# Output projection of the last two pairs of heads taken one head later, in a two-layer transformer kernel

## What is computed

```python
# layer 1 attention: x seen as B = 4 sequences of S tokens, H = 32 heads of 128
q = jnp.einsum('bsd,de->bse', hidden_states, wq).reshape(B, S, H, DQ)
scores = jnp.einsum('bqhd,bkhd->bhqk', q[..., :DN], k) * scale     # causal mask
probs = jax.nn.softmax(scores, axis=-1)
attn = jnp.einsum('bhqk,bkhd->bqhd', probs, v).reshape(B, S, H * DV)
return jnp.einsum('bse,ed->bsd', attn, wo)
# after it
x = _layernorm(x + attention(x))
x = _layernorm(x + L1_ffn(x))      # dense matrix plus gated low-rank experts
```

## Time and profile before

| | |
|---|---|
| time, median of 3 runs | 1513.86 us (1513.7 to 1514.61) |
| time of the profiled execution | 1514.25 us |
| its span | 1512.4 us |
| TensorE busy in the span | 1447.8 us, 96% |
| VectorE, ScalarE, GpSimd busy | 1021.7, 899.0, 797.5 us |
| mean granted TensorE clock | 0.985 of full |
| heads 30 and 31 with the epilogue | about 1382 to 1438 us of the span |
| last stage | from 1438.28 us to the end |

### The profile page before, as it was taken

One profiled execution on the slowest core, in us unless ns is written; L12 is line 12 of the kernel. 1 busy time (PEld: TensorE's weight loads), 2 busy tenths in 40 slices (PEclk: granted clock), 3 DMA queues, 4 the chain that ended last, 5 costly groups with the idle time before them and its releaser, 6 DMA issues. The chain is left out here.

```text
span 1512.4 us, 30701 instructions
## 1 busy us (share of the span) xinstructions
PE 1447.8 (96%) x8801; PEld 1267.2 (84%) x8801; DVE 1021.7 (68%) x2484; ACT 899.0 (59%) x2445; POOL 797.5 (53%) x891
## 2 busy tenths in 40 slices
PE   6999999999599988999999999999999999999797
PEld 5898898988377767988898898899889889889686
DVE  3788888888496866566656656656665566566665
ACT  3787878888355536555655655655566555556521
POOL 3455555555241226775756657566565665654421
PEclk9999999999899999999999999999999999999999
DMA  4223232322245410101010010100101011010201
GB/s 166 66 70 88 67 86 72 82 77 65 69 133 161 129 44 28 57 29 56 28 55 28 28 55 28 55 28 30 54 28 55 28 38 45 28 42 14 77 15 42
DMA packets 56196, 88.62 MB, mean 59 GB/s; under 512 B 6112, under 2 KB 31200, under 8 KB 56160
## 3 DMA queue, kind: packets, MB, share of 16 engines
q1 hardware_dynamic: 56160, 88.16, 19.4%
HBM read 77.66 MB, written 2.10 MB: 53 GB/s over the span
## 5 line engine op out<-in xcount | busy, mean ns | idle before, releaser
L1292 POOL TENSOR_TENSOR c_qk<-g_y,c_qk 128x512 fp32r<-128x512 f32 x96 | 124.1, 1293 | 149.5 <-ACT c_qk L1386 149.5
L466 POOL TENSOR_TENSOR h_pr<-h_pr,h_rinv 128x512 f32<-128x512 f32 x128 | 133.3, 1041 | 132.0 <-DVE h_rinv L557 129.6
L1170 POOL TENSOR_TENSOR b_sw_lo<-b_slots,b_sw_hi 128x512 fp32r<-128x512 f32 (+1 forms) x128 | 148.7, 1162 | 10.2
L1168 POOL CAST b_sw_hi<-b_slots 128x512 fp32r<-128x512 f32 (+1 forms) x128 | 73.0, 570 | 134.9 <-DMA b_slots<-in_w_qk 124.0
L98 PE MATMUL c_bv<-b_wv_hi,g_xT_hi 128*128 128x256 f32 x504 | 141.0, 280 | 0.0
L99 PE MATMUL c_bv<-b_wv_lo,g_xT_hi 128*128 128x256 f32 x504 | 140.8, 279 | 0.0
L100 PE MATMUL c_bv<-b_wv_hi,g_xT_lo 128*128 128x256 f32 x504 | 140.7, 279 | 0.0
L1386 ACT ACTIVATE c_qk<-g_y 128x512 fp32r<-128x512 f32 x96 | 61.0, 636 | 106.1 <-DVE g_y L1512 75.2
L496 ACT ACTIVATE h_pr<-h_bs,h_nmax 128x256 f32<-128x256 f32 x256 | 119.0, 474 | 6.4 <-DVE h_nmax L552 3.0
L1486 DVE TENSOR_TENSOR c_bo<-c_bo,g_wo 128x128 f32<-128x128 f32 x128 | 38.4, 300 | 119.0 <-ACT g_wo L1363 119.0
L1353 ACT ACTIVATE c_pr<-c_pr,c_rinv 128x128 f32<-128x128 f32 (+1 forms) x256 | 102.4, 450 | 8.2 <-DVE c_rinv L1476 8.2
(11 more groups left out here) (303 smaller groups left out, 5237.0 us busy)
## 6 DMA issues: line engine op xcount, KB each, us to landing
f_wi<-in_w_ffn SPq DMA_DIRECT2D x66, 256.0 KB, 2.6
b_slots<-in_w_qk SPq DMA_DIRECT2D x64, 256.0 KB, 2.8
h_part<-in_w_ffn SPq DMA_DIRECT2D x32, 264.0 KB, 2.7
h_o_mix<-h_o_hi SPq DMA_DIRECT2D x64, 128.0 KB, 2.2
b_raw_v<-in_w_v SPq DMA_DIRECT2D x16, 512.0 KB, 4.5
b_raw_o<-in_w_o SPq DMA_DIRECT2D x16, 512.0 KB, 4.4
a_w<-in_w_head SPq DMA_DIRECT2D x32, 225.0 KB, 2.6
b_ffn_w<-in_w_ffn SPq DMA_DIRECT2D x4, 576.0 KB, 6.8
```

Source lines behind the costliest of these rows:

```text
L466: pool.tensor_tensor(pr[b][:, :, :], pr[b][:, :, :], rinv[b][:, :][:, :, None].to_broadcast([P, 2, S]), ALU.mult)\
L1168: pool.tensor_copy(self.sw[0][:, a:b], self.slots[:, a:b]).then_inc(self.s_whi, 1)
L1170: pool.tensor_tensor(self.sw[1][:, a:b], self.slots[:, a:b], f32(self.sw[0][:, a:b]), ALU.subtract)\
L1292: pool.tensor_tensor(lo, src, f32(hi), ALU.subtract).then_inc(s_sumlo, 1)
```

## The change

All 16 output tiles of the last two pairs are taken later, in one sequence numbered `n` = 0 to 15 (`late_out`, `late_add`, `late_tile`). Tiles 0 and 1 (of pair 14) come in step 3 of head 30, two in each step of head 31 (2 to 7 of pair 14, 8 and 9 of pair 15), and the six others of pair 15 in the epilogue. Steps 0 to 2 of head 30 have no output tile. The banks rotate over three (`bv`, `by`, `bx`), and a tile waits for the addition of the tile three before it.

As pair 14's result is still needed while pair 15's is written, head 30 writes its result to a new place, `o_last`, which lies under the former `slots`; its first write waits until GpSimd has split the last projection weights. The last pair's output weights go to the buffers of the value weights (`split_last_o`), once all values are made, no longer behind the tiles of pair 14.

ScalarE's `ffn1_hi` pieces move: one after step 1, two after step 2, two after step 3 of head 31, none in the epilogue. VectorE's epilogue puts the statistics of token tiles 0 to 3 between the additions.

```diff
+        last = k.under("o_last", [P, 2, T], F32R)
+        self.o_last = (last[:, 0, :], last[:, 1, :])
...
+    def split_last_o(self, pool, used):
+        pool.wait_ge(self.s_in["o"], 16 * NG)
+        pool.wait_ge(*used)
+        plain(pool, self.g["tick"])
+        hi, lo = self.ws["v"]
+        pool.tensor_copy(hi[:, :], self.raw["o"][:, :]).then_inc(self.s_vohi["v"], 1)
+        pool.wait_ge(self.s_vohi["v"], NG + 1)
+        pool.tensor_tensor(lo[:, :], self.raw["o"][:, :], f32(hi[:, :]), ALU.subtract).then_inc(self.s_volo["v"], 1)
...
+        def home(gr, hd):
+            return self.o_last if is_last_pair(gr) and hd == 0 else tuple(x[:, hd, :] for x in oT)
+        def late_tile(n):
+            return NG - 2 + n // NT, n % NT, (bv, by, bx)[n % 3]
...
-                    if hd == 1 and has(gr, NG):
+                    if hd == 1 and is_last_pair(gr):
+                        self.split_last_o(pool, (s_vmm, 4 * NG))
+                    elif hd == 1 and has(gr, NG):
                         self.split(pool, "o", gr, [(s_omm, 8 * gr)])
...
+                    if to is self.o_last and b == 0:
+                        act.wait_ge(s_wlo, 4 * NH)
...
                         if is_last(gr, hd) and t:
-                            ffn1_hi(act, self.ffn_raw, t - 1)
+                            for c in ((0,), (1, 2), (3, KC))[t - 1]:
+                                ffn1_hi(act, self.ffn_raw, c)
                 def epilogue():
                     out_rest(NSTEP - 1, 3)
-                    outs(NSTEP - 1, 1, 3)
-                    for c in (KC - 1, KC):
-                        ffn1_hi(act, self.ffn_raw, c)
+                    outs(NSTEP - 1, home(NG - 1, 1), 3)
...
-                        if is_last(gr, hd) and t:
+                        if is_last_pair(gr) and (hd == 1 or t == 3):
                             for i in range(2):
-                                j = 2 * t - 2 + i
-                                add_out(8 * gr + j, j, (bx, by)[i])
+                                late_add((2 + 2 * t if hd else 0) + i)
...
                     out_sum(NSTEP - 1, 3)
-                    outs(NSTEP - 1, 1, 3)
-                    for j in range(4):
-                        after.stats(dve, j, (s_oadd, 8 * (NG - 1) + j + 1))
+                    stats(0)
+                    outs(NSTEP - 1, home(NG - 1, 1), 3)
+                    stats(1)
+                    for j in (2, 3):
+                        late_add(NT + j)
+                        stats(j)
                     after.spread(dve, 0)
-                    for i in range(2):
-                        add_out(NT * NG - 2 + i, NT - 2 + i, (bx, by)[i])
+                    for j in late:
+                        late_add(NT + j)
...
                         def tile(i):
+                            if is_last_pair(gr):
+                                if hd == 1 or t == 3:
+                                    late_out((2 + 2 * t if hd else 0) + i)
+                                return
...
-                            if is_last(gr, hd) and t:
-                                n = 8 * gr + 2 * t - 2 + i
-                                pe.wait_ge(s_oadd, n - 1)
-                                pe.wait_ge(s_olo, s)
-                                out(gr, 2 * t - 2 + i, (bx, by)[i])
...
+                def late_out(n):
+                    gr, j, bank = late_tile(n)
+                    if n == 0:
+                        pe.wait_ge(s_vlo, 4 * NG)
+                    elif n == 1:
+                        pe.wait_ge(s_sum, 3 * NH)
+                    elif n == 2:
+                        pe.wait_ge(s_klo, NH)
+                    else:
+                        pe.wait_ge(s_oadd, NT * (NG - 2) + n - 2)
+                    if is_last_pair(gr):
+                        pe.wait_ge(s_olo, NSTEP - 3 + j // 2)
+                    out(gr, j, bank)
+
                 def epilogue():
-                    pe.wait_ge(s_olo, NSTEP)
-                    for i in range(2):
-                        pe.wait_ge(s_oadd, NT * NG - 3 + i)
-                        out(NG - 1, NT - 2 + i, (bx, by)[i])
+                    for j in range(2, NT):
+                        late_out(NT + j)
```

More of the change, by code:

```diff
@@ L1256, in is_last, with is_last_pair @@
             return isinstance(gr, int) and (gr, hd) == (NG - 1, 1)
+        def is_last_pair(gr):
+            return isinstance(gr, int) and gr == NG - 1
+        def home(gr, hd):
+            return self.o_last if is_last_pair(gr) and hd == 0 else tuple(x[:, hd, :] for x in oT)
+        def late_tile(n):
+            return NG - 2 + n // NT, n % NT, (bv, by, bx)[n % 3]
         turned = [bo[0], bo[1], bt, bs[1]]
@@ L1363, in out_rest, with outs @@
                     act.activation(o1, bo[t % 2][:, 2 * P:3 * P], ACT.Identity).then_inc(s_orest, 1)
-                def outs(s, hd, b):
+                def outs(s, to, b):
                     act.wait_ge(s_osum, s + 1)
-                    act.activation(oT[0][:, hd, b * S:(b + 1) * S], bo[b % 2][:, 0:S], ACT.Identity)\
+                    if to is self.o_last and b == 0:
+                        act.wait_ge(s_wlo, 4 * NH)
+                    act.activation(to[0][:, b * S:(b + 1) * S], bo[b % 2][:, 0:S], ACT.Identity)\
                        .then_inc(s_ohi, 1)
@@ L1432, in unit @@
                         if has(s - 1, NSTEP):
-                            outs(s - 1, hd if t else 1 - hd, (t - 1) % 4)
+                            outs(s - 1, home(gr, hd if t else 1 - hd), (t - 1) % 4)
                         if has(s + 1, NSTEP):
@@ L1486, in out_sum, with outs @@
                     dve.tensor_tensor(out, out, o1, ALU.add).then_inc(s_osum, 1)
-                def outs(s, hd, b):
+                def outs(s, to, b):
                     dve.wait_ge(s_ohi, s + 1)
                     tok = slice(b * S, (b + 1) * S)
-                    dve.tensor_tensor(oT[1][:, hd, tok], bo[b % 2][:, 0:S], f32(oT[0][:, hd, tok]), ALU.subtract)\
+                    dve.tensor_tensor(to[1][:, tok], bo[b % 2][:, 0:S], f32(to[0][:, tok]), ALU.subtract)\
                        .then_inc(s_olo, 1)
@@ L1585, in unit @@
                             inverse(s + 1, (t + 1) % 4)
-                        if hd == 0 and has(gr - 1, NG):
+                        regular = hd == 0 and has(gr - 1, NG) and not is_last_pair(gr)
+                        if regular:
                             add_out(8 * (gr - 1) + 2 * t, 2 * t, bv)
@@ L1591, in unit, with late_add, stats @@
                             total(h + 1, t)
-                        if hd == 0 and has(gr - 1, NG):
+                        if regular:
                             add_out(8 * (gr - 1) + 2 * t + 1, 2 * t + 1, bv if t < 3 else by)
-                        if is_last(gr, hd) and t:
+                        if is_last_pair(gr) and (hd == 1 or t == 3):
                             for i in range(2):
-                                j = 2 * t - 2 + i
-                                add_out(8 * gr + j, j, (bx, by)[i])
+                                late_add((2 + 2 * t if hd else 0) + i)
+                def late_add(n):
+                    _, j, bank = late_tile(n)
+                    add_out(NT * (NG - 2) + n, j, bank)
                 def epilogue():
+                    def stats(j):
+                        after.stats(dve, j, (s_oadd, NT * (NG - 1) + j + 1))
                     out_sum(NSTEP - 1, 3)
-                    outs(NSTEP - 1, 1, 3)
-                    for j in range(4):
-                        after.stats(dve, j, (s_oadd, 8 * (NG - 1) + j + 1))
+                    stats(0)
[4 more added lines that the diff above has]
+                        stats(j)
                     after.spread(dve, 0)
-                    for i in range(2):
-                        add_out(NT * NG - 2 + i, NT - 2 + i, (bx, by)[i])
+                    for j in late:
+                        late_add(NT + j)
                 sweep(dve, prologue, unit, epilogue)
@@ L1664, in out @@
                 def out(gr, j, bank):
-                    pe.wait_ge(s_volo["o"], gr + 1)
+                    if is_last_pair(gr):
+                        ws = self.ws["v"]
+                        pe.wait_ge(s_volo["v"], NG + 1)
+                    else:
+                        ws = self.ws["o"]
+                        pe.wait_ge(s_volo["o"], gr + 1)
                     for hd in range(2):
-                        o = tuple(z[:, hd, j * P:(j + 1) * P] for z in oT)
-                        w = tuple(z[:, hd * HID:(hd + 1) * HID] for z in self.ws["o"])
+                        o = tuple(z[:, j * P:(j + 1) * P] for z in home(gr, hd))
+                        w = tuple(z[:, hd * HID:(hd + 1) * HID] for z in ws)
                         m = matmul3(pe, bank[:, :], o, w, hd == 0, hd == 1)
```

## The result

The changed kernel takes 1505.42 us, median of 8 runs (1502.1 to 1510.16), against 1514.64 for the kernel before (8 runs, 1513.48 to 1516.29). The ratio is 0.9941 with a 95% interval of 0.9926 to 0.9956: 9 us faster. The prediction was 1503.8 us in a range of 1500.8 to 1508.4. The profiled execution took 1505.38 us, its span is 1503.5.

The account below looks back on a forecast made before the run. Head 30 is bound by TensorE, head 31 by the chain of waits through a step. 18.6 + 17.9 + 8.2 + 1.25 = 45.9 us instead of 55.9, 10.0 less: 1503.8 us, range 1500.8 to 1508.4.

Parts of the forecast that it names:

- A: Likeliest case: the summed terms hold, 10.0 us less, 1503.8 us, own range 1501.5 to 1506; chance 0.70.
- Head 30: Steps 0 to 2 without tiles at 4.33 us, step 3 at 4.2, stalls 1.4: 18.6 us, before 25.33.
- The wait for `key_lo`: Step 2 of head 30: head 31's scores wait 0.9 us for key_lo, late in the chain.
- The small stalls of ScalarE's queue: Steps 0 to 2 of head 30: ScalarE's chain, 4.58 us against TensorE's 4.33, stalls of about 0.1, 0.2 and 0.2 us.
- Head 31: Two tiles per step fill the idle times; steps 16.2 us, with waits from ffn1_hi pieces 17.9 us.
- The clock in head 31: TensorE's fall to half speed after the 1.82 us wait, 2.6 us lost, should be gone.
- The clock at the stage's start: Start of the last stage: half-speed fall taken as unchanged, at nothing; ends -2.5 us and +0.9 us.
- The sum: First scores of head 30 to first instruction of the last stage: 45.9 us instead of 55.9, 10.0 less.
- B: Rival: ScalarE's queue and ffn1_hi pieces cost more in both heads; 5.4 us gained, 1508.4 us; chance 0.12.
- D: Rival: waits only move, head 30's thinned steps stand as long as the tiles did; 1512.0 us; chance 0.03.
- E: Rival: slower, TensorE falls to half speed repeatedly in the thinned heads; 1517.4 us with four more stretches; chance 0.02.
- C: Rival: the summed terms hold and the clock stays full at the last stage's start; 1501.3 us; chance 0.13.

Follow-up runs that it names:

- 6: hi_moved: changed kernel with ffn1_hi pieces one after step 0, two after step 3 of head 31, two in the epilogue; 1505.11 us, ratio 0.9925.
- 11: best2: changed kernel, one epilogue tile moved to head 30's step 2, epsilon on ScalarE, ffn1_hi pieces after steps 0, 2, 3 (two) and in epilogue; 1501.61 us.
- experiment 3: before_hi: kernel before, with only the ffn1_hi pieces moved to the changed kernel's places; 1512.36 us, ratio 0.9977.
- experiment 2: before_warm: kernel before, with six unread matmuls added in the empty step 0 of head 31; 1513.86 us, ratio 0.9994.
- experiment 1: The changed kernel run again, unedited; 1504.19 us, ratio 0.9933.
- hi_early: Changed kernel with ffn1_hi pieces one after step 0, one after step 1, two after step 3 of head 31, one in the epilogue; 1502.97 us, ratio 0.993.
- wo_shared: Changed kernel without own buffers for the last pair's output weights, split only when pair 14's eight tiles are done; 1509.81 us, ratio 0.9967.
- tile_hi: 7: on top of 6, one output tile more in step 2 of head 30, one fewer in the epilogue; 1504.62 us, ratio 0.9934.

## Why the prediction was right

Its likeliest case, A, is what happened, and the range held the time. Point by point:

- *Head 30*, 18.6 us predicted: 18.20 (1384.72 to 1402.92). The wait for `key_lo` was sized 0.9 us; step 2 is 0.9 us longer than step 0, and VectorE's `key_lo` (L1544) ends at 1398.53, 0.1 us before the scores start. The small stalls of ScalarE's queue were 0.05 us, not 0.1 to 0.2 in each step, although its chain was sized rightly: from one `out_rest` to the next (1390.10 to 1394.64) it takes 4.54 us, 4.58 computed. The slack took up more of it than I had allowed.
- *Head 31*, 17.9 us: 17.69 (1402.92 to 1420.61). Two errors cancel here. The piece after step 1 cost 0.3 us, not 0.7, and the two after step 2 cost 0.85, not 1.0; the steps themselves took 16.55 us, not 16.2. Experiments 6 and 11 show that these were the pieces: with them elsewhere the waits are gone.
- *Epilogue*, six tiles, 8.2 us: 8.24. *From the last tile to the stage*, 1.25: 1.22. GpSimd no longer sets the end; experiment 3 prices that at 1.35 us, the prediction had 1.9 for the whole end.
- *The clock in head 31*, 2.6 us: 2.43 in experiment 2, against a profile of before with a long fall. The size of this term in other executions is open.
- *The clock at the stage's start*, taken as unchanged with ends at -2.5 and +0.9: it fell for 3.4 instead of 6.8 us, 0.7 us saved in the profile of the changed kernel. Without a fall the last stage takes 71.9 us, 2.2 less than the 74.1 of before, near the predicted end of 2.5. The Trainium skill, TensorE: Matmul & The Clock Gate, Part 1, says that where the clock changes varies between runs of one kernel. The traces agree: 6.8, 3.4 and 0 us at half in kernels whose last stage is the same.
- *The sum* 45.9 us is 45.35. The terms give 10.5 us, the ratio 9 (6.7 to 11.2 by its interval). With the 0.7 us of the last stage the two profiles give 11.2, at the upper end of it.
- *From the sum to the time.* 1505.42 is 1.6 us above 1503.8. Half of it is the starting point: the kernel before has a median of 1514.64 in 8 runs, and I had started from 1513.86 in 3. The other half is the gain, 9.2 us by the medians against 10.0. That the number came so near is in part luck: single runs of the changed kernel lie up to 8 us apart, as experiment 1 shows, and my sum took no account of what varies ahead of head 30.

Rivals B, D and E are out: ScalarE's pieces did not add up, steps 0 and 1 of head 30 fell to 4.3 us and step 2 to 5.2, and neither head has a half-speed part. C came true by half in the profiles (3.4 instead of 6.8 us at half), not in the time.

**What I had overlooked.** The prediction gave VectorE 0.6 us to spare in the epilogue (0.67 in the profile) and did not look at L779, the addition of epsilon to four variances. It waits for GpSimd, and the kernel before showed it already:

```profile
1435.20 0.55 DVE L779 TENSOR_SCALAR g_mv<-g_mv 128x4 f32<-128x4 f32 x1
1433.05 3.90 POOL L1829 TENSOR_TENSOR b_ffn_lo<-b_ffn_w,b_ffn_hi 128x1152 fp32r<-128x1152 f32 x2 [2.45 <-ACT b_ffn_hi L1822]
```

The durations of L779 and what GpSimd did:

| kernel | L779 on VectorE, us | it ends at | GpSimd's running subtraction ends at |
|---|---|---|---|
| before_hi, hi_early | 0.17, 0.17 | 1435.50, 1425.12 | idle |
| before, before_warm | 0.55, 0.55 | 1435.75, 1435.31 | 1435.72, 1435.28 |
| changed kernel | 0.31 | 1426.33 | 1426.30 |
| wo_shared | 1.28 | 1430.64 | 1430.62 |
| hi_moved | 1.40 | 1427.16 | 1427.14 |
| tile_hi | 2.09 | 1425.51 | 1425.49 |

In the six kernels of the table that have GpSimd busy there, the instruction ends 0.02 to 0.03 us behind GpSimd's, and with GpSimd idle it takes 0.17 us. The same instruction runs five more times in each of the 14 profiles, every time with GpSimd idle, and takes 0.17 us in all 70. The repeated run of the changed kernel and the one with two banks (0.29 and 0.32 us) are like the changed kernel's row. In the changed kernel this costs only 0.14 us, by luck: GpSimd's last piece ends as VectorE arrives, and VectorE still idles 0.67 us before its last addition. 6 and 7 moved VectorE and GpSimd's pieces against each other and gave half or all of their gain back.

The Trainium skill, SBUF — State Buffer, section SBUF: two separate sides, says that VectorE and GpSimd share one pair of ports as an exclusive lock, held for a whole instruction. It names VectorE's 2-port modes and its instructions with two SBUF inputs as those concerned, and counts `tensor_scalar` among the instructions that can run in such a mode (section Who interferes with whom). The traces agree with the lock. That this one, with a single input of 4 columns, ran in such a mode no run here shows; the runs show only that it is held back, and that VectorE's aggregations before it are not (0.15 to 0.18 us each with GpSimd busy as with GpSimd idle), nor its additions from PSUM (0.66 to 0.69 us in either case).

## What to carry to other kernels

Work that depends on nothing recent is worth most where a chain of waits has lost its filling: the same 16 tiles, pair 14's taken three steps later and pair 15's two, made 56 us into 45. Of the 10.5 us, 1.35 belong to the moved weight copies and up to 2.4 to the clock, and neither the own buffers for weights (4 us) nor the third bank (1 us) could be left out. Before packing such a place more tightly, look for short VectorE instructions on SBUF beside long GpSimd instructions: the duration of a tiny instruction in the profile tells whether it is being held back. And give each auxiliary piece a place by the slack of that place: one copy cost 0.3 us after step 1 in the changed kernel and nothing after step 2 in best2.

## What the runs showed of the hardware

- A VectorE `tensor_scalar` of 128x4 took from 0.17 to 2.09 us, by how much of a running GpSimd subtraction (1.3 or 2.69 us long) was left.
- 1.37 us of useless matmuls in an idle time of 2.06 us made the attention 2.43 us faster in one profile, in which the clock stayed up. Waits of 1.82 us in the middle of the heads were followed by a fall for 6.8 and 3.4 us, one of 2.58 us by a fall for 3.4 us; waits of 0.70, 1.36, 1.41 and 1.71 us were not. At the start of the last stage idle times of 1.66 and 1.41 us had falls for 0, 3.4 and 6.8 us.
- The time at half speed ahead of head 30, in stages that no edit touched, differs by 17 us between profiles (23.9 to 40.9), and the beginning of head 30 by 6.4 us. Single runs of one kernel differ by up to 8 us.
